# Causal masks of three attention stages: block rows in the q and k stacks, and 64x64 triangles added in each head's half of the array

## The reference

```
L0 cross-attention part: causal self scores, and scores against a context of 64 tokens
L2 attention, REPETITIONS = 3 times over:
    scores = einsum('bthd,bshd->bhts', q, k * scale) + mask      # mask: NEG = -10000 where s > t
    attn = softmax(scores); q <- the attention's result
L2 feed-forward part, _mha with rope:
    scores = where(tril, q k^T / sqrt(8), -inf); softmax; @ v
```

## Time and profile before

| | |
|---|---|
| median of 3 runs | 4342.0 us (4332.91 to 4346.76) |
| the profiled execution, first to last instruction | 4397.2 us |
| PE / DVE / ACT busy, share of the span | 78% / 64% / 47% |
| mean granted clock of TensorE, share of full speed | 0.867 |
| maxima and scores: slots with a causal mask | 128 in s1, 384 in s6, 128 in s8 |

### The profile page before, as it was taken

The page is one execution under the profiler, slowest core; times in us unless marked ns, Lnnn a source line. Parts: engine busy times, 40 slices in busy tenths (PEclk is TensorE's granted clock), DMA queues, the critical chain, the costliest instruction groups (busy, mean ns, idle before and its releaser), DMA issues. The chain is left out here.

```text
span 4397.2 us, 86721 instructions
## 1 busy us (share of the span) xinstructions
PE 3437.7 (78%) x30670; PEld 2240.3 (51%) x30670; DVE 2793.4 (64%) x7633; ACT 2088.0 (47%) x4656; POOL 1182.3 (27%) x2276
## 2 busy tenths in 40 slices
PE   6886888896888658759998989677993588869882
PEld 2443554463555338734454545343553466669882
DVE  5884675264786575547676777476865468954453
ACT  2664665232443435426666766443660234335551
POOL 2322221011111234540101110133322422234555
PEclk9987998797998679969999999787995599879996
DMA  5323331033221322230202021223322230122322
GB/s 89 64 35 55 56 56 22 15 95 49 32 39 14 57 70 67 76 58 21 42 24 38 25 38 27 37 53 54 55 35 65 80 92 19 59 70 85 91 80 62
DMA packets 320664, 231.40 MB, mean 53 GB/s; under 512 B 45491, under 2 KB 305168, under 8 KB 320188
## 3 DMA queue, kind: packets, MB, share of 16 engines
q1 hardware_dynamic: 306444, 198.57, 22.8%
q0 software_dynamic: 12928, 26.50, 2.1%
q10 hardware_dynamic: 864, 0.79, 0.1%
HBM read 68.43 MB, written 55.53 MB: 28 GB/s over the span
## 5 line engine op out<-in xcount | busy, mean ns | idle before, releaser
L1373 ACT ACTIVATE PT<-ps 128x512 f32<-128x512 f32 (+1 forms) x1600 | 812.2, 559 | 468.7 <-PE ps L1433 223.0
L1323 DVE TENSOR_REDUCE M<-ps 128x2 f32<-128x512 f32 x1024 | 655.3, 684 | 236.1 <-PE ps L1307 209.3
L1286 PE MATMUL ps<-SKB 49*128 49x256 bf16 (+2 forms) x3584 | 422.6, 275 | 131.7 <-DVE M L1323 53.5
L1320 DVE TENSOR_REDUCE M<-ps 128x3 f32<-128x384 f32 x768 | 390.6, 550 | 180.5 <-PE ps L1304 119.5
L1468 PE MATMUL ps<-PT,VA 128*9 128x256 f32 (+1 forms) x7168 | 449.8, 370 | 1.3 <-ACT PT L1373 1.0
L3847 ACT ACTIVATE SKB<-ps,SKB 128x128 f32<-128x128 f32 x1032 | 295.5, 372 | 279.6 <-PE ps L3765 194.6
L1413 PE MATMUL ps<-SKB 51*128 51x256 bf16 (+2 forms) x3584 | 362.6, 267 | 59.4 <-DMA SKB<-MT 37.0
L3911 DVE COPY SKB<-SKB 128x1028 f32 (+1 forms) x258 | 186.6, 723 | 287.0 <-PE ps L3774 167.7
L1286 PEld LDWEIGHTS ps<-SKB 48*128 48x128 bf16 (+1 forms) x3584 | 137.8, 95 | 427.9 <-issue 131.0
L3774 PE MATMUL ps<-SKB 128*128 128x128 f32 x2064 | 288.7, 285 | 29.9 <-ACT SKB L3847 22.1
L3765 PE MATMUL ps<-SKB 128*128 128x128 f32 x2064 | 293.4, 288 | 0.0
(11 more groups left out here) (497 smaller groups left out, 6720.8 us busy)
## 6 DMA issues: line engine op xcount, KB each, us to landing
SKB<-HH SPq DMA_DIRECT2D x1212, 64.0 KB
SKB<-HH SPq DMA_DIRECT2D x576, 32.0 KB
PT<-L_sorted_rows SPq DMA_DIRECT2D x258, 64.0 KB
L_sorted_results<-SKB SPq DMA_DIRECT2D x258, 64.0 KB
SKB<-in_L3f_w SPq DMA_DIRECT2D x32, 256.0 KB
L_sorted_rows<-TV SPq DMA_DIRECT2D x2, 4032.0 KB, 29.4
SKB<-scratch SPq DMA_DIRECT2D x2, 2048.0 KB, 11.0
SKB<-in_L1f_w SPq DMA_DIRECT2D x16, 256.0 KB
```

The costliest lines, as they stand in the source:

```text
L1286: k = e.matmul(self.mx_bank(m + i)[:, o:o + n], K.QS[self.set(c)][64 * i:64 * i + rows, s, 256 * bb + 128 * qt:256 * bb + 128 * qt + 128], ...
L1320: k = e.tensor_reduce(K.M3[n % 2][:, hh, 0:3], mx[:, 0:384].rearrange("p (a k) -> p a k", a=3), axis=AX.X, op=ALU.max)
L1323: k = e.tensor_reduce(K.M3[n % 2][:, hh, 0:2], mx.rearrange("p (a k) -> p a k", a=2), axis=AX.X, op=ALU.max)
L1373: e.activation(K.PT[:, x % 4, n * i:n * i + n], self.st_bank(x, i)[:, 0:n], ACT.Exp, bias=0.0, scale=self.scale).then_inc(*self.exp.inc())
```

## The change

Three edits go together.

- The blocks of the mask off the diagonal, now in units of 64 tokens, become three more constant rows of both stacks in "causal" and "add" (`mrow` 51 in both): row j of the q stack is one for queries of block j, row j of the k stack is the mask's value for keys of blocks behind j. They come with the rows of ones out of a DRAM table of 13 rows that the DVE writes at the start into a corner of X (`dve_patterns`) and 13 DMAs store (`sp_table`). Every masked stage, and s3, loads its rows into each of the three sets of stacks with the first three pairs (`sp_stack_rows`), in place of `sp_mask_rows` and `sp_ones`.
- What stays of the mask are 64x64 triangles on the diagonal, two for each 128x128 block. `pe_triangle` adds those of one head for both diagonal blocks with an operand of 64 partitions, the head's own half: a matmul of 128 columns, two for each head and kind of scores.
- In masked modes `pe_max_mask` moves ahead of `pe_exp` in the slot.

```diff
+    def dve_patterns(self, e):
+        rows = K.X[0:1, 0:13, :].bitcast(BF16)
...
-        self.mrow = 49 if mode == "add" else 48
+        self.mrow = 51 if self.masked else 48
...
+    def sp_stack_rows(self, e, kind, c):
+        K, i = self.K, self.set(c)
+        if kind == "q":
+            at, n, dst = 10, 3 * self.masked, K.QS[i]
+        elif self.masked:
+            at, n, dst = 5 * (self.mode == "add"), 5, K.KS[i]
+        else:
+            at, n, dst = 3, 2 * (self.begin is None), K.KS[i]
+        for par in range(2 if n else 0):
+            r = 64 * par + 48
+            e.dma_start(dst[r:r + n, :, :].bitcast(F32), K.row_table[at:at + n, :].rearrange("r (a k) -> r a k", a=8)
+                        ).then_inc(self.rows_in[i].sem, 16)
...
+        if self.masked:
+            for sub in range(2):
+                for i in range(2):
+                    k = self.pe_triangle(e, self.mx_bank((16 + 4 * self.cross) * u + 2 * s + i), i, sub, 0)
+                    if sub == 1:
+                        k.then_inc(*self.mx.inc())
...
-                k = e.matmul(mx.rearrange("p (a k) -> p a k", a=4)[:, 0:4:3, :], K.idb[:, :], twice(self.mask[:, 0:128]),
-                             start=False, stop=True)
...
+    def pe_triangle(self, e, bank, i, sub, turned):
+        K = self.K
+        if self.mode == "causal":
+            blocks = bank.rearrange("p (a k) -> p a k", a=2)
+        else:
+            blocks = bank.rearrange("p (a k) -> p a k", a=4)[:, 0:4:3, :]
+        part = slice(64 * i, 64 * i + 64)
+        tri = K.tri[part, 2 * (self.mode == "add") + turned:2 * (self.mode == "add") + turned + 1, :].to_broadcast([64, 2, 64])
+        return e.matmul(blocks[:, :, 64 * sub:64 * sub + 64], K.idh[sub][part, :], tri, start=False, stop=sub == 1)
...
         if maxima:
             self.pe_max(e, *maxima)
+        if maxima and self.masked:
+            self.pe_max_mask(e, *maxima)
         if scores:
             self.pe_exp(e, *scores)
-        if maxima:
+        if maxima and not self.masked:
             self.pe_max_mask(e, *maxima)
         if scores:
             self.pe_exp_mask(e, *scores)
...
+        if self.begin and g == 30:
+            self.begin.sp_table(e)
```

More of the change, by code:

```diff
@@ L241, in sp_context @@
         e.dma_start(K.g8[:, :], A["L2f_g"]).then_inc(self.late.sem, 16)
+        for i, words in enumerate((A["c_maskq"][0:64, 0:32], A["c_maskk"][0:64, 0:32], A["c_addm"][0:64, 0:32],
+                                   A["c_addm"][0:64, 128:160])):
+            for par in range(2):
+                e.dma_start(K.tri[64 * par:64 * par + 64, i, :].bitcast(F32), words).then_inc(self.late.sem, 16)
     def pool(self, e):
@@ L982, in __init__ @@
         self.scale_q = RS8 / self.scale
-        self.rows_in = K.ev("mask_rows_in", 1, 16 * 18) if mode == "add" else None
-        self.ones_in = K.ev("ks_ones_in", 1, 16 * 6) if again else None
+        self.rows_in = [K.ev(f"stack_rows{i}", 1, 16 * (4 if self.masked else 0 if begin else 2)) for i in range(3)]
         nff = len(self.ff_splits) - 2 * cross
@@ L1165, in sp_split @@
                 self.qk_free(e, key)
+            if step == 0 and key < 3:
+                self.sp_stack_rows(e, kind, key)
             self.stack(e, n, SPLIT_Q, K.QS[self.set(key)], 64, self.stack_steps(step), (0,) if n < self.shared else (0, 1))
@@ L1419, in pe_exp_mask @@
         K, mode = self.K, self.mode
[L1420 removed]
+        x = self.nx * u + s
+        if self.masked:
+            for sub in range(2):
+                for i in self.heads(x):
+                    k = self.pe_triangle(e, self.st_bank(x, i), i, sub, 1)
+                    if sub == 1:
+                        k.then_inc(*self.st.inc())
+        if mode != "bias":
             return
[L1422 removed]
         for i in self.heads(x):
             hh = 8 * i + s
[L1425 to L1434 removed]
+            e.matmul(self.st_bank(x, i)[:, 256:384], K.idf[:, :], self.bias.KB[:, hh, 0:128], start=False, stop=True
+                     ).then_inc(*self.st.inc())
     def dve_bias(self, e, u, s):
@@ L2297, in sp_slot @@
                 self.later.load(e)
-            if self.next is not None and self.next.ones_in:
-                self.next.sp_ones(e)
         if self.beside is not None:
```

105 lines of the change are left out of this document (44 added, 61 removed).

## The result

Median 4288.5 us in four runs (4279.3 to 4290.6) against 4342.2 for the kernel before, measured beside it: ratio 0.9881, 95% interval 0.9863 to 0.9899, 54 us less. The forecast was 83 us less, 4259, with a range of 4190 to 4325: the direction was right, and the time lies in the range, but a third of the gain did not come. The changed kernel was measured once more in another set of runs, where the kernel before stood at 4390 us: ratio 0.9897 (0.9877 to 0.9916).

The account below looks back on a forecast made before the run. It took s6's PE as full, with a chain through the SP queue just as long. Terms: -47 (s6), -15 (s1), -26 (s8), +5 (start) = -83 us, off 4342 giving 4259; range 4190 to 4325.

Parts of the forecast that it names:

- The slot: PE slot in masked stages: 0.72 us, or 0.80 before another array shape, against 1.09; 2.3 us of PE saved per unit.
- rivals 2, 3 and 4: Triangle pairs take 0.10 us: 4302 (chance 0.12); heads' triangles not concurrent: 4340 (0.05); each triangle awaits its weights: 4440 (0.06).
- The chain of s6: 29 units paced through SP's queue: 4.74 us head shrinks 0.5, 11.07 us of shifts, DMAs and landing stay; 14 us saved.
- A PE with more idle time loses some clock ... I give back 2: In s6, lost clock from a less busy PE costs 2 us, leaving 47 of 49 us saved.
- Free units of s6: Some 15 units of s6 that wait for no stack of a repetition: 2.0 us saved each, 30 us.
- There the PE's 2.3 us would show: In some 15 s6 units without a stack wait, the PE's saving shows; 2.0 each taken because of units with a block's end.
- Stalls: Three s6 units wait on a backlogged SP queue; the stall stays, the six slots behind save 1.8 us each, 5 us.
- s8: 13 units go from 17.05 to 15.0 us, 2.0 saved each: 26 us, bounds 13 and 37.
- 31.7 - 4.6: PE time of a pair of s8 units less the saving of both: 27.1 us.
- The maskless s0 unit lies 1.4 us over its PE time: That 1.4 us, added to 13.55 us of PE, gives an s8 unit of 15.0 us.
- s1: 2.1 us saved per pair of units, seven pairs, 15 us; the wait for the shift stays; bounds 5 and 32.
- The start: Memsets, casts and 13 table stores ahead of s0, first rope product near 17.5 us: +5 us, bounds 0 and 14.

Follow-up runs that it names:

- e11: The changed kernel as it is, measured and profiled again in another set of runs; ratio 0.9897 to the kernel before.
- e9: Changed kernel plus 18 throwaway matmuls ahead of the wait for the stacks in places 4 to 8 of each group of twelve units of s6; ratio 0.9852.
- e10: Changed kernel with two of twelve stack DMAs per repetition in s6 and four of 24 per pair of sequences in s1 issued by the ACT; ratio 0.9751.
- e8: Changed kernel with its start work doubled: patterns made twice, 26 table rows stored instead of 13; ratio 0.9938, 27 us slower than the changed kernel.
- e7: Changed kernel with every triangle added twice in all three masked stages; ratio 0.9949, 4321 us.

## Why the prediction was right in part

**The slot.** Forecast 0.72 us and 0.80 ahead of another shape; measured 0.68, 0.77 ahead of a values product and 0.94 ahead of the turn L726 (PE of a unit 12.3 us, forecast 12.5). Pairs of 128 columns on the two halves do run together, at 0.055 to 0.06 us, although one load of a triangle's identity takes 101 ns, as long as the whole one of the earlier trace rows:

```profile
L1347 PEld LDWEIGHTS ps<-tri,idh 64*128 64x128 bf16 x5120 | 282.4, 101 | 33.3
```

That the load of 64 rows is no shorter agrees with the Trainium skill (TensorE: Matmul & The Clock Gate, LDWEIGHTS), and that it did not matter decides against rivals 2, 3 and 4 of the prediction. Stacks of 51 and 53 rows cost nothing.

**The chain of s6.** Right: 15.2 us instead of 15.8 in a unit at full clock; the shifts go out 4.12 us after the start instead of 4.76, 0.64 against the 0.5 taken, and the 11.07 us behind are what they were.

**The clock.** Here the sum failed. The step "A PE with more idle time loses some clock ... I give back 2" was mis-sized: 28 units of the chain x 0.64 = 18 us were won at its head, and their mean is 16.2 us as before. Over s6 the clock went from 0.97 to 0.91, (0.09 - 0.03) x 790 = 47 us of full speed not granted, and since the slow piece lies at the head of the unit, it lies on the chain: the shifts go out up to 1.5 us later. 12 of the 20 chain units have such a piece (a 13th is long by a late landing). So the 14 us forecast for the chain came to nothing. In places 4 to 9 of the changed kernel's trace 17 starts follow a wait of 1.87 to 2.90 us, and in 16 of these units the clock falls; one wait of 2.05 us had no fall behind it (start at 2630.14), and none followed the seven waits of 0.43 to 1.62 us. In e11 one of 1.94 us had none either. Before the change the longest waits in these places were 1.20, 1.33 and 1.53 us, without a fall. Two pieces of 6.8 us left waits of only 1.2 us behind them, and the next units ran at speed. e9 gives the price: 11.5 us come back when the gap is filled. The Trainium skill (TensorE: Matmul & The Clock Gate, HAM oscillation — how this bites in real kernels) describes such a loop of DMA wait and slow restart. This trace agrees with the loop; its waits, 1.9 to 2.9 us, are shorter than those of the page's example. I had read the stalled unit's 0.87 as the exception and not as what most chain units would become.

**Free units of s6.** Forecast 2.0 each, measured 1.0. Place 11 saved 1.9 (16.5 to 14.6), place 0 saved 1.5 and place 2 saved 1.7, but place 1 became 1.0 longer (16.0 to 17.0). The step "There the PE's 2.3 us would show" took all four for PE-bound. In place 1 the scores now wait 2.13 us for their shift, where the wait was 0.19 us before the change; in place 2 the maxima wait 1.69 us for the DVE. In six of these eight units a half-speed piece begins, in the two shown less than 1.4 us behind the end of the wait:

```profile
2150.72 0.39 PE L1451 MATMUL ps<-SKB 53*128 53x256 bf16 x4 [2.13 <-DMA SKB<-MT]
...
2163.85 0.39 PE L1313 MATMUL ps<-SKB 51*128 51x256 bf16 x3 [1.69 <-DVE M L1361]
```

With 15 x 1.0 + 28 x 0 + 3 x 0.7 the parts give the 17 us of the windows. **Stalls**: they stayed, as said; their units gained 0.7 us each where 1.8 were forecast.

**s8.** Forecast 26 us, measured 13. A pair takes 31.7 us where 30.0 was forecast and 34.1 stood. Two terms failed. The PE of a pair at full clock is busy 28.1 us instead of the 27.1 of "31.7 - 4.6", so it saved 3.6 us and not 4.6. And the pair lies 3.6 us over that, not the 2.9 of "The maskless s0 unit lies 1.4 us over its PE time": the wait for the DVE in the unit with a block's end, first row, before the change, is still there in the second, after it.

```profile
3162.08 0.34 PE L1286 MATMUL ps<-SKB 48*128 48x128 bf16 x3 [1.36 <-DVE M L1320]
...
3140.25 0.34 PE L1313 MATMUL ps<-SKB 51*128 51x128 bf16 x3 [1.49 <-DVE M L1358]
```

Two new half-speed pieces (clock 0.97 to 0.95) fall in the two units that became longer, by 1.6 and 0.9 us.

**s1.** Forecast 15, measured 12 from its start to that of s3 (637.4 to 625.0 us), 8.5 of it in s1's own units (profiles of kernels that leave s1 as changed have 328.0 to 335.0 us for them, so this is good to some 4 us). As forecast the wait for the shift stays; it is now preceded by one for the stacks of the cross queries (the first of the stage aside, 1 us in two waits before and 7 us in six now), and a pair without a slow piece takes 42.0 us against 44.2:

```profile
572.34 0.61 PE L793 MATMUL ps<-SKB 96*128 96x128 bf16 x8 [0.95 <-DMA SKB<-HH]
...
582.11 0.34 PE L1451 MATMUL ps<-SKB 53*128 53x256 bf16 x4 [2.24 <-DMA SKB<-MT]
```

What holds the pairs of s1 in the end stays open: e10 took 2.6 us per pair from the queue, and nothing came of it.

**The start.** The first rope product stands at 18.28 us (forecast 17.5), the 13 stores take 8.18 us (8.6), the first scores stand at 75.13, before they would be late (85). But +5 came out as -1: s0's first maxima stand 3.3 us later (54.6 against 51.3), yet s1 began at 376.2 us against 377.3, since s0's second unit took 15.0 us instead of 20.0, in part undone by the third (17.5 instead of 14.0). Nothing in the forecast said so: these 6 us are luck. e8 shows that it was close.

Added up, the stretches that the change touches give -1 (start), -12 (s1), +2 (s3), -17 (s6), -1 (s6 to s8), -13 (s8): 42 us in the pair of traces, beside 54 and 46 in the two comparisons of medians. Of the missing gain 30 us are in s6, 13 in s8 and 3 in s1; the start gave 6 back. Mechanism and order of size were right for the slot and for the chain's head. The bounds did worse than the total: s6's 17 us lie outside the 28 to 110 given for it and the start's -1 outside 0 to 14, and s8's 13 on its lower bound. The total lies in its range because that range is wider than these bounds taken together.

## What to carry to other kernels

Before a saving on a full engine is counted, look for the chain that is nearly as long, and take its head alone; then ask what the engine does in the gap that opens. On this chip a gap of some 2 us in front of the critical piece made the PE run that very piece at half speed, so that the 18 us won at the chain's head were lost again; filling the gap with throwaway work gave 11.5 back, and shortening the chain that makes it, 50. A change of order and a change of shape are to be priced together: here the new order alone cost 29 us, the new shape alone won 28, and both won 54.

## What the runs showed of the hardware that I had not expected

- 18 extra matmuls ahead of each of 20 units made s6 11.5 us shorter, and 3000 extra ones all over it cost 1.5 us of 783 (e9, e7).
- The PE's clock fell from 1.00 to 0.50 behind 16 of 17 single waits of 1.87 to 2.90 us between chain units, and behind none of the seven of 0.43 to 1.62 us there.
- Two profiles of one and the same kernel differ by 20 and 34 us in the two stretches with the experts (572.0 and 592.1, 1090.3 and 1124.1 us): a difference of spans between two kernels has to be cut by stages before it is read.
